# A decoder block in fp32 on one Trainium2 core: a new hand-written order of steps on every engine, new users of the PSUM banks, and 17 constant matrix products in place of 44

## The chip, the cores and the metric

The kernel runs on one core of a Trainium2 chip. The metric is the device time of one execution in microseconds (us), as the median of a few runs. The engines are PE (TensorE, matrix products; PEld is its weight load), DVE (VectorE), ACT (ScalarE), POOL (GpSimd) and SP (SyncE, which here issues all DMAs). They run side by side, each takes its own instructions in the order of the program, and they wait for one another on semaphores.

## What is computed

Four batches of 512 tokens with 128 features go through three residual stages:

```python
x = x + _L0_attn_ref(_layernorm(x), gamma)     # softmax(-gamma * |yi - yj|^2) @ y
x = x + _L0_xattn_ref(_layernorm(x), ctx, ctx, ...)   # 16 heads of 8, 154 keys, a bias linear in the distance
x = x + _L0_ffn_ref(_layernorm(x), ...)        # router: the best 2 of 8 experts, each 128x128
```

## The kernel before, in words

**Steps.** The work is cut into named steps. `name:b.k` is part k of batch b. Each engine's part of a step is a small function: `keys`, `maxima` and so on in the block of that engine. The functions wait on semaphores for what they read.

- Stage 1, a batch: DVE takes `stats1` (L981, L984), POOL turns a variance into a factor (`rstd1`: L695, L697; one call for batch 0, one for batches 1 to 3), DVE writes `y1` (L989), PE turns it (`y1T`, L1249: four 128x128 transposes, the "turned block"), ACT copies it to SBUF. POOL makes the squared norms (`squares`, L705 to L720, again batch 0 and then batches 1 to 3), PE turns them (`sqT`), ACT copies. PE forms four blocks of distances (`dist`, two fp32 instructions of 512 columns, L1263, and a bf16 one, L1266). DVE takes the row maximum (L1005), ACT clips (L851), DVE finishes `rowmax`, ACT takes the exponential (`soft`, L857), PE turns it (`probs`, L1214), ACT copies, and PE multiplies (`self`, L1279). DVE adds it to the residual and takes the next statistics (`gather`: L1019, L1023, L981, L984).
- Stage 2: `rstd2` (POOL), `y2` (DVE, L989), `y2T` and `query` (PE, L1286 and L1294, copied by ACT), `split` (a query in three bf16 pieces, three instructions; batch 0 on DVE, the others on POOL), then `qout` and `qin`: DMAs to DRAM and back into `qs`. The keys go the same way once: `keys` (ACT L871; DVE L1043 to L1049), `kout`, `kin`. `maxima` are 22 groups a batch: PE forms scores of three heads (L1316), DVE takes the maxima (L1091). `mcat` (DVE), `mT` (PE, ACT), `mout` and `min` (DMA) bring them back as three more rows of `qs`. `scores` (PE L1344, L1340; ACT exponential L919) are 20 a batch, `values` (PE L1371, L1367), `divide` (PE, DVE L1122, L1124), `aoT`, `wo` (PE L1390; DVE L1132 and the third statistics). `key_values` and `tail_values` write the values of all batches into `vm` and `vt`, which POOL clears first (`zeros`, L679 to L687).
- Stage 3: `rstd3`, `y3` (L989), `y3T`, `route` (PE L1404; DVE L1150 to L1166), `mask` (PE, ACT), masked tokens (`select`: batch 0 on POOL, L816, eight instructions, from `mask_all`, which comes over `eout` and `ein`; the others on DVE, L1186, from a product on PE, `spread`, L1421), `experts` (PE L1440) and `store`.

**Order.** The dictionary `ORDER` (L60) writes out by hand, for each engine, the list of its steps; `walk` (L238) goes through it. So an engine that waits in a step holds up all that is behind it in its list. Batches overlap: while DVE reduces `maxima` of batch 1, PE already works on `scores` of batch 0.

**Banks.** `TURNS` (L173) lists, for each of the eight PSUM banks, its users in order. Before a step writes, `turn` (L1204) lets PE wait until the user ahead of it in the list has been read.

**Constant products.** `WARM` (L232) gives numbers of products (L1210, 128x512 bf16 of a tile of ones, their results never read) that `turn` issues after its own wait and ahead of a step: 28 ahead of `y1T:0.0`, 4 ahead of `sqT:0.0`, 2 ahead of `probs:0.0`, 3 ahead of `y1T:3.0`, 2 ahead of `maxima:0.0`, 4 ahead of `probs:3.0`, 1 ahead of `scores:0.0`: 44 in all.

```python
for _ in range(WARM.get(f"{name}:{b}.{k}", 0)):
    mm(at(name, b, k)[:, :], idle[:, 0:P], idle[:, :], start=True, stop=True)
```

## Time and profile before

| what | us |
|---|---|
| median of 3 runs | 182.98 |
| the runs | 182.98, 184.85, 182.34 |
| span of the profiled execution, first to last instruction | 182.3 |
| busy in it: PE, PEld, DVE, ACT, POOL | 173.4, 123.6, 150.5, 105.8, 60.7 |

The profiled execution is one of its own; its time is its span and next to nothing around it, 0.04 us under the fastest of the runs shown and 0.7 us under their median. A row of the timeline gives the start, the duration, the engine, the line, the operation, output and inputs, shapes and a count, and in brackets the idle time of the engine before it with what ended it. Durations of PE overlap, since matmuls are pipelined: how far two starts lie apart tells more than one duration.

### The profile page before, as it was taken

How to read it: one execution, taken by the hardware profiler on the slowest of the kernel's cores; microseconds unless marked ns; L12 is line 12 of the kernel's file. 1: busy time of each engine (PE TensorE's matmuls, PEld its weight loads, DVE VectorE, ACT ScalarE, POOL GpSimd, SP SyncE). 2: the span in 40 equal slices, each digit the busy share in tenths (PEclk: the TensorE clock that was granted, in tenths of full speed). 3: DMA queues.
4: the chain of work that ended last, by engine and by line, in shares of the span. 5: the costliest groups of instructions: out<-in, count | busy, mean ns of one | idle time of the engine just before them, and what ended most of it. 6: DMA issues, size and time to landing. Idle time of an engine off the chain costs nothing.

```text
span 182.3 us, 4382 instructions
## 1 busy us (share of the span) xinstructions
PE 173.4 (95%) x1514; PEld 123.6 (68%) x1514; DVE 150.5 (83%) x433; ACT 105.8 (58%) x219; POOL 60.7 (33%) x123
## 2 busy tenths in 40 slices
...
GB/s 99 335 153 0 4 213 50 176 103 192 79 162 162 156 161 129 159 125 92 198 130 62 14 7 12 8 5 50 192 4 0 4 58 2 16 45 0 32 0 86
DMA packets 20003, 15.84 MB, mean 87 GB/s; under 512 B 1621, under 2 KB 18133, under 8 KB 19833
## 3 DMA queue, kind: packets, MB, share of 16 engines
...
q8 instruction: 12, 0.20, 0.5%
...
## 4 chain that ended last, share of the span: by engine, by line
PE 72%; DVE 19%; issue 3%; ACT 3%; POOL 1%; ACTq 0%; DVEq 0%
PE bank L1440 15%; DVE nm L1091 9%; PE bank L1371 8%; PE bank L1344 7%; PE bank L1316 6%; PE bank L1214 6%; PE bank L1263 6%; PE bank L1210 5%; PE bank L1279 4%; DVE y L989 3%; PE bank L1421 3%; PE bank L1340 2%; PE bank L1367 2%; ACT w L857 2%; PE bank L1390 2%
## 5 line engine op out<-in xcount | busy, mean ns | idle before, releaser
L1091 DVE TENSOR_REDUCE nm<-bank 128x3 f32<-128x462 f32 (+1 forms) x88 | 48.6, 614 | 0.8 <-PE bank L1316 0.6
L919 ACT ACTIVATE pt<-bank 128x512 f32<-128x512 f32 x80 | 43.3, 604 | 3.8 <-PE bank L1344 2.7
L1440 PE MATMUL bank<-ewT,ym 128*128 128x128 f32 x256 | 32.5, 277 | 0.0
L1440 PEld LDWEIGHTS bank<-ewT,ym 128*128 128x128 f32 x256 | 30.3, 192 | 0.2
L1316 PE MATMUL bank<-ks,qs 99*128 99x308 bf16 (+1 forms) x170 | 25.2, 262 | 0.0
L1344 PE MATMUL bank<-qs,ks 105*128 105x256 bf16 (+1 forms) x96 | 21.6, 309 | 0.0
L1316 PEld LDWEIGHTS bank<-ks,qs 99*128 99x128 bf16 x170 | 15.1, 98 | 8.3 <-DVE nm L1091 2.2
L1186 DVE TENSOR_TENSOR ym<-bank,y3T 128x512 f32<-128x512 f32 x24 | 15.1, 684 | 4.9 <-PE bank L1421 4.9
L798 POOL TENSOR_SCALAR ve<-mv 128x2 f32<-128x2 f32 (+1 forms) x6 | 1.3, 210 | 50.2 <-DVE mv L984 50.0
L1371 PE MATMUL bank<-pt,vm 128*32 128x256 f32 (+1 forms) x192 | 17.3, 456 | 0.0
L1263 PE MATMUL bank<-y1Tg,y1T 128*128 128x512 f32 x32 | 16.6, 601 | 0.3 <-ACT y1Tg L837 0.3
L989 DVE TENSOR_SCALAR y<-xs,mv,rs 128x128 f32<-128x128 f32 x48 | 16.2, 390 | 0.7 <-POOL rs L772 0.4
L1279 PE MATMUL bank<-y,pT 128*128 128x128 f32 x128 | 16.5, 278 | 0.2
L1279 PEld LDWEIGHTS bank<-y,pT 128*128 128x128 f32 x128 | 15.4, 191 | 1.2 <-DVE xs L1023 0.5
L1210 PE MATMUL bank<-idle 128*128 128x512 bf16 x44 | 13.6, 459 | 2.2 <-DVE idle L972 1.5
L851 ACT ACTIVATE w<-bank,snsq,sgn 128x512 f32<-128x512 f32 x16 | 12.3, 774 | 5.2 <-DVE rm L1005 5.2
L1005 DVE TENSOR_REDUCE rm<-bank 128x1 f32<-128x512 f32 x16 | 10.6, 681 | 4.8 <-PE bank L1266 4.8
L857 ACT ACTIVATE w<-w,nrb,sgn 128x512 f32<-128x512 f32 x16 | 12.9, 811 | 2.9 <-DVE nrb L1014 2.9
L824 ACT ACTIVATE maskT<-bank 128x256 bf16<-128x256 bf16 (+1 forms) x6 | 2.6, 454 | 19.6 <-PE bank L1440 14.0
L1344 PEld LDWEIGHTS bank<-qs,ks 105*128 105x128 bf16 x96 | 8.6, 97 | 7.5 <-issue 4.0
L981 DVE BATCH_NORM_STATS2 st<-xs 128x6 f32<-128x128 f32 x48 | 11.0, 282 | 1.1 <-DMA xs<-in_x_dram 0.6
L824 ACT ACTIVATE pT<-bank 128x512 f32<-128x512 f32 x16 | 9.6, 602 | 2.1 <-PE bank L1214 1.9
...
## 6 DMA issues: line engine op xcount, KB each, us to landing
...
```

The source lines that it names most:

```text
L857: nc.scalar.activation(w[b][:, t, :], w[b][:, t, :], ACT.Exp, bias=nrb[b][:, t:t + 1], scale=sgn[:, :], accum_out=den[b][:, t:t + 1]).then ...
L919: nc.scalar.activation(pt[:, n % RING, :], at("scores", b, i)[:, :], ACT.Exp).then_inc(exps, 1)
L989: v.tensor_scalar(y[:, t, :], src[:, t, :], mv[:, t, 0:1], rs[:, t:t + 1], ALU.subtract, ALU.mult).then_inc(s, 1)
L1091: v.tensor_reduce(nm[b][:, n:n + heads], at("maxima", b, g)[:, 0:heads * J].rearrange("p (s j) -> p s j", s=heads), AX.X, ALU.max, negate= ...
L1186: v.tensor_tensor(ym[:, e:e + per, c], masks, y3T[b][:, c].unsqueeze(1).broadcast_to([P, per, n]), ALU.mult).then_inc(masked_last, 1)
L1210: mm(at(name, b, k)[:, :], idle[:, 0:P], idle[:, :], start=True, stop=True)
L1263: mm(at("dist", b, t)[:, :], y1T[b][:, tile(t)], y1Tg[b][:, :], start=True, stop=False)
L1279: last = mm(at("self", b, p)[:, tile(t)], pT[b][:, t, u, :], y1[b][:, u, :], start=(u == 0), stop=(u == T - 1))
L1316: last = mm(at("maxima", b, g)[:, at_ * J:(at_ + heads) * J], qs[b][0:MAXROW, a, tile(t)], ks[b][0:MAXROW, a, s:s + heads, 0:J], start=Tru ...
L1344: last = mm(bank_[:, :], ks[b][0:TOP, h // 2, h % 2, 0:JM], qs[b][0:TOP, h // 2, c], start=True, stop=True)
L1371: last = mm(dst, vm[:, b, h, :], e, start=(r == 0), stop=(r == ROUNDS - 1), skip_group_check=True)
L1440: last = mm(at("experts", b, p)[:, tile(t)], ym[:, e, tile(t)], ewT[:, e, :], start=False, stop=(e == E - 1), skip_group_check=True)
```

## The change

Only `ORDER`, `TURNS` and `WARM` change. The steps are the same ones, as many on each engine, with the same instructions. The core of the diff, each part cut:

```diff
     "sync": """
-        x:0.0 gamma:0.0 x:1.0 x:2.0 k_rows:0.0 cols:0.0 x:3.0 context:0.0 weights:0.0 experts:0.0 k_rows:1.0
...
+        x:0.0 gamma:0.0 x:1.0 k_rows:0.0 k_rows:1.0 k_rows:2.0 k_rows:3.0 context:0.0 cols:0.0 experts:0.0 x:2.0 x:3.0
+        weights:0.0 q_rows:0.0 kout:0.0 kout:1.0 kin:0.0 kout:2.0 kin:1.0 kout:3.0 kin:2.0 kin:3.0 qout:0.0 qout:0.1
...
     "gpsimd": """
-        setup:0.0 gamma:0.0 rstd1:0.0 squares:0.0 bias:0.0 rstd1:1.0 weights:0.0 zeros:0.0 squares:1.0
-        rstd2:0.0 y1g:1.0 rstd2:0.1 y1g:2.0 x1b:0.0 rstd2:1.0 rstd2:1.1 y1g:3.0 split:1.0 x1b:1.0 split:1.1
...
+        zeros:0.0 setup:0.0 rstd1:0.0 gamma:0.0 squares:0.0 bias:0.0 weights:0.0 expert_bias:0.0 rstd1:1.0 squares:1.0
+        y1g:1.0 rstd2:0.0 y1g:2.0 rstd2:0.1 x1b:0.0 rstd2:1.0 rstd2:1.1 x1b:1.0 y1g:3.0 split:1.0 split:1.1 rstd2:2.0
...
     "scalar": """
+        table:0.0 y1T:0.0 sqT:0.0 dist:0.0 dist:0.1 dist:0.2 keys:0.0 soft:0.0 soft:0.1 probs:0.0 keys:0.1 probs:0.1
+        soft:0.2 dist:0.3 y1T:1.0 soft:0.3 sqT:1.0 probs:0.2 sqT:2.0 probs:0.3 dist:1.0 y2T:0.0 y1T:2.0 dist:1.1
+        dist:1.2 sqT:3.0 dist:1.3 y2T:0.1 soft:1.0 query:0.0 soft:1.1 query:0.1 probs:1.0 soft:1.2 soft:1.3 probs:1.1
...
     "vector": """
-        dist:0.3 rowmax:0.0 y1:1.0 keys:0.0 key_values:0.0 gather:0.0 key_values:0.1 key_values:0.2
-        key_values:0.3 y2:0.0 gather:0.1 y1:2.0 dist:1.0 y2:0.1 split:0.0 dist:1.1 dist:1.2 dist:1.3 rowmax:1.0
-        keys:0.1 split:0.1 dist:2.0 dist:2.1 dist:2.2 gather:1.0 dist:2.3 rowmax:2.0 y2:1.0 gather:1.1 y1:3.0
...
+        rowmax:0.0 keys:0.0 y1:1.0 keys:0.1 gather:0.0 key_values:0.0 dist:1.0 key_values:0.1 y2:0.0 key_values:0.2
+        y1:2.0 gather:0.1 dist:1.1 dist:1.2 key_values:0.3 dist:1.3 y2:0.1 rowmax:1.0 dist:2.0 tail_values:0.0
+        dist:2.1 split:0.0 dist:2.2 split:0.1 dist:2.3 rowmax:2.0 gather:1.0 gather:1.1 y2:1.0 y1:3.0 maxima:0.0
...
+        maxima:3.16 y3:0.0 maxima:3.17 maxima:3.18 maxima:3.19 maxima:3.20 divide:2.0 divide:2.1 maxima:3.21 mcat:3.1
+        route:0.0 divide:2.2 y3:1.0 wo:2.0 divide:2.3 y3:2.0 route:1.0 divide:3.0 wo:2.1 divide:3.1 wo:3.0 y3:2.1
...
     "tensor": """
-        scores:3.17 experts:0.1 experts:0.2 y3T:2.0 scores:3.18 wo:3.0 mask:1.0 scores:3.19 experts:0.3
...
+        start:0.0 y1T:0.0 sqT:0.0 dist:0.0 dist:0.1 dist:0.2 dist:0.3 keys:0.0 keys:0.1 key_values:0.0 probs:0.0
+        tail_values:0.0 probs:0.1 self:0.0 y1T:1.0 self:0.1 probs:0.2 sqT:1.0 sqT:2.0 sqT:3.0 probs:0.3 dist:1.0
+        self:0.2 self:0.3 y2T:0.0 dist:1.1 y1T:2.0 dist:1.2 dist:1.3 dist:2.0 query:0.0 y2T:0.1 dist:2.1 dist:2.2
+        query:0.1 probs:1.0 probs:1.1 dist:2.3 self:1.0 probs:1.2 probs:1.3 self:1.1 self:1.2 self:1.3 maxima:0.0
...
+        scores:3.12 scores:3.13 scores:3.14 values:3.3 scores:3.15 values:3.4 values:3.5 values:3.6 mask:1.0
+        experts:0.0 scores:3.16 scores:3.17 experts:0.1 experts:0.2 scores:3.18 scores:3.19 divide:3.1 experts:0.3
...
 WARM = {
-    "y1T:0.0": 28, "sqT:0.0": 4, "probs:0.0": 2, "y1T:3.0": 3, "maxima:0.0": 2, "probs:3.0": 4,
-    "scores:0.0": 1,
+    "y1T:0.0": 17,
 }
```

In `TURNS` each of the eight lists is written anew; the first users of each bank stay `y1T:0.0`, `sqT:0.0`, `dist:0.0` to `dist:0.3`, `kp:0.0` and `kp:0.1`. In the middle of the lists, `mcat:0.0` stands behind `maxima:1.0` and `y2:2.0` on DVE, where it stood ahead of `maxima:1.0`; `wo:1.0` stands ahead of `maxima:3.16`, where it stood behind `route:0.0`.

## Rows read from the trace of the kernel before

**Rows 1.** The page: busy time, share of the span, instructions

```profile
PE 173.4 (95%) x1514; PEld 123.6 (68%) x1514; DVE 150.5 (83%) x433; ACT 105.8 (58%) x219; POOL 60.7 (33%) x123
```

**Rows 2.** Busy time by stretches: stretch, length, engines, granted clock, DMA share, GB/s

```profile
10.48:13.78 3.30, 3.03 (x17) 1.80 (x16) 0.00 (x0) 1.67 (x3) 3.14 (x6) 1.00 0.12 47
...
45.96:62.88 16.92, 16.65 (x140) 11.90 (x140) 16.78 (x39) 10.13 (x23) 6.55 (x11) 1.00 0.49 131
...
74.23:119.00 44.77, 44.77 (x449) 26.65 (x450) 42.40 (x111) 36.70 (x75) 11.97 (x24) 1.00 0.28 77
...
140.40:182.30 41.90, 38.52 (x346) 35.56 (x346) 28.75 (x79) 5.03 (x13) 2.77 (x6) 1.00 0.08 26
```

**Rows 3.** The timeline: constant products on PE and their weight loads

```profile
1.50 9.13 PE L1210 MATMUL bank<-idle 128*128 128x512 bf16 x28 [1.50 <-DVE idle L972]
...
7.03 0.15 PEld L1210 LDWEIGHTS bank<-idle 128*128 128x128 bf16 x1 [0.28 <-issue]
...
7.46 2.69 PEld L1210 LDWEIGHTS bank<-idle 128*128 128x128 bf16 x13 [0.28 <-issue]
...
46.04 0.82 PE L1210 MATMUL bank<-idle 128*128 128x512 bf16 x3 [0.68 <-DVE y L989]
```

**Rows 4.** The timeline of the head, POOL, DVE, PE and ACT

```profile
5.35 1.04 POOL L697 TENSOR_TENSOR rs<-ve,minus_half 128x4 f32<-128x4 f32 x1
...
6.86 1.08 DVE L989 TENSOR_SCALAR y<-xs,mv,rs 128x128 f32<-128x128 f32 x4
...
10.48 0.60 PE L1249 MATMUL bank<-ident,y 128*128 128x128 f32 x4
...
12.20 0.59 ACT L824 ACTIVATE sqT<-bank 3x512 bf16<-3x512 bf16 x1
...
12.43 1.10 PE L1263 MATMUL bank<-y1Tg,y1T 128*128 128x512 f32 x2 [0.27 <-ACT y1Tg L837]
```

**Rows 5.** POOL's stretches: setup, squares:0.0, rstd1:1.0, zeros, squares:1.0, expert_bias

```profile
0.78:2.15 1.37, 1.12 (x7) 1.00 0.00 0
6.46:9.10 2.64, 2.06 (x9) 1.00 1.02 355
10.39:12.97 2.58, 2.50 (x3) 1.00 0.19 73
13.99:17.90 3.91, 3.62 (x10) 1.00 0.00 0
17.86:21.95 4.09, 3.52 (x10) 1.00 0.01 4
76.01:80.21 4.20, 3.64 (x11) 1.00 0.17 45
```

**Rows 6.** The timeline: one POOL cast of few elements, alone and beside DVE

```profile
8.35 0.20 POOL L716 CAST sqp<-nsr 128x4 bf16<-128x4 f32 x1
...
19.71 0.80 DVE L1045 TENSOR_TENSOR ym<-ym,mask_all 128x616 f32<-128x616 f32 x1
19.81 0.80 POOL L716 CAST sqp<-nsr 128x12 bf16<-128x12 f32 x1
```

**Rows 7.** The timelines of DVE and PE ahead of the first maxima

```profile
40.39 0.61 DVE L1023 SCALAR_TENSOR_TENSOR xs<-bank,rd,xs 128x128 f32<-128x128 f32 x2 [0.74 <-PE bank L1279]
...
43.79 1.35 PE L1316 MATMUL bank<-ks,qs 99*128 99x308 bf16 x12
```

**Rows 8.** The timeline of the late stretch, PE, DVE and POOL

```profile
122.96 0.40 PE L1214 MATMUL bank<-ident,maskp 128*128 128x128 bf16 x4
...
130.65 9.57 POOL L816 TENSOR_TENSOR ym<-mask_all,y3T 128x512 f32<-128x512 bf16 x8 [3.77 <-DMA mask_all<-e_scratch]
...
132.91 2.36 DVE L989 TENSOR_SCALAR y<-xs,mv,rs 128x128 f32<-128x128 f32 x2
...
135.29 1.11 PE L1440 MATMUL bank<-ewT,ym 128*128 128x128 f32 x8
...
140.43 0.38 PE L1214 MATMUL bank<-ident,maskp 128*128 128x128 bf16 x4 [0.92 <-DVE maskp L1166]
```

More of the change, by code:

```diff
@@ L77 @@
+        y1g:1.0 rstd2:0.0 y1g:2.0 rstd2:0.1 x1b:0.0 rstd2:1.0 rstd2:1.1 x1b:1.0 y1g:3.0 split:1.0 split:1.1 rstd2:2.0
+        split:2.0 rstd2:2.1 x1b:2.0 rstd2:3.0 split:2.1 rstd2:3.1 x1b:3.0 split:3.0 split:3.1 rstd3:0.0 rstd3:1.0
+        rstd3:2.0 select:0.0 select:0.1 select:0.2 select:0.3 select:0.4 select:0.5 select:0.6 select:0.7 rstd3:2.1
+        rstd3:3.0 rstd3:3.1
     """,
     "scalar": """
-        table:0.0 y1T:0.0 sqT:0.0 dist:0.0 dist:0.1 dist:0.2 keys:0.0 soft:0.0 soft:0.1 probs:0.0 probs:0.1
@@ L99 @@
+        scores:3.19 aoT:3.0 y3T:2.0 mask:1.0 y3T:2.1 values:3.2 values:3.3 aoT:3.1 mask:2.0 mask:2.1 y3T:3.0 y3T:3.1
+        mask:3.0 mask:3.1
     """,
     "vector": """
[L101 to L104 removed]
@@ L221 @@
-    """,
-    """
-        kp:0.1 dist:1.1 probs:1.0 probs:1.2 maxima:0.0 query:1.0 y2T:1.1 maxima:0.14 probs:2.3 probs:3.0
-        self:3.0 self:3.1 maxima:2.2 y2T:3.1 query:3.1 scores:1.2 maxima:2.16 scores:1.11 maxima:2.20
-        maxima:3.2 maxima:3.6 scores:2.1 scores:2.5 scores:2.8 maxima:3.16 scores:2.15 maxima:3.21 scores:3.0
-        mask:0.0 pv:2.3 scores:3.11 scores:3.15 aoT:3.0 wo:3.0 route:2.0 spread:2.0 spread:2.4 route:3.1
-        spread:3.3
+        y1T:0.0 vp:0.0 dist:2.1 y2T:1.0 query:1.0 maxima:0.10 probs:2.2 maxima:0.21 probs:3.1 maxima:1.5
@@ new lines @@
+        scores:0.0 scores:0.4 maxima:1.14 maxima:1.17 scores:0.15 divide:0.0 maxima:2.5 scores:1.0 maxima:2.12
+        maxima:2.15 maxima:2.19 scores:1.15 aoT:0.0 maxima:3.8 maxima:3.12 wo:0.0 wo:1.0 maxima:3.19
+        scores:2.17 aoT:2.0 y3T:1.0 aoT:2.1 scores:3.12 mask:1.0 spread:1.1 experts:1.0 route:3.0 spread:2.7
+        spread:3.4
+    """,
+    """
+        sqT:0.0 probs:0.0 probs:0.2 self:0.1 dist:2.0 y1T:3.0 maxima:0.5 self:2.0 y2T:2.0 query:2.0 maxima:1.1
+        probs:3.2 maxima:1.8 scores:0.7 scores:0.10 y2T:3.1 maxima:1.21 scores:0.19 query:3.1 scores:1.1
+        maxima:2.14 maxima:2.17 maxima:2.21 divide:1.0 maxima:3.7 maxima:3.10 pv:2.0 scores:2.13 scores:2.15
+        maxima:3.21 scores:3.2 pv:3.0 scores:3.13 scores:3.16 divide:3.1 route:2.0 mask:2.0 spread:2.3
+        experts:2.1 spread:3.6
@@ new lines @@
+    """,
+    """
+        dist:0.2 self:0.0 y2T:0.0 dist:1.3 probs:1.0 probs:1.3 probs:2.0 maxima:0.7 dist:3.1 maxima:0.15
+        maxima:0.20 probs:3.0 probs:3.3 self:3.1 maxima:1.13 maxima:1.16 scores:0.13 maxima:2.0 maxima:2.3
+        maxima:2.8 scores:1.3 scores:1.7 scores:1.11 scores:1.12 scores:1.14 scores:1.18 maxima:3.5 scores:2.2
+        maxima:3.13 scores:2.7 scores:2.11 maxima:3.20 scores:2.19 mT:3.1 wo:2.0 route:1.0 scores:3.11
+        scores:3.15 scores:3.18 wo:3.0 spread:1.0 spread:1.4 y3T:3.0 spread:2.5 spread:3.0 experts:3.0
```

219 lines of the change are left out of this document (94 added, 125 removed).

## The prediction

> **What bounds the kernel now.** I read the page's busy times first. PE is busy 173.4 of 182.3 us, DVE 150.5 [rows 1], so two engines could each be the limit, and the next view, busy time by stretches, has to say where. From 45.96 to 62.88 (the maxima of batch 0 up to their last) DVE is busy 16.78 of 16.92 us; from 74.23 to 119.00 PE is busy throughout, while DVE has 42.40 of 44.77; from 140.40 on DVE has slack (28.75 of 41.90) and PE has the experts to work through [rows 2]. The reader is to see a kernel that is bound by DVE up to about 70 us and by PE behind that. A new order can win only what these two now wait. Third, the timeline of the head: DVE has written y1 at 7.94 (6.86 + 1.08), but PE turns it at 10.48, since 28 constant products are ahead of it [rows 3, 4]. From there the chain goes through ACT to the first distance product at 12.43.
>
> **Part 1, the products ahead of the turned block.** The weight loads tell their pace: those at 7.03 and 7.46 are 0.43 us apart, and the 13 from 7.46 on take 2.69 us, 0.215 from start to start [rows 3]. So 14 products run at 0.43 (1.50 to 7.46) and 14 at 0.215. 512 columns in 0.43 us are the 1.2 GHz level and in 0.215 the 2.4 GHz level; the granted clock reads 1.00 in each stretch of [rows 2], which is the 2.4 GHz level. Seventeen products take 14 x 0.43 + 3 x 0.215 = 6.7 us and end at 8.2. That alone would bring the turned block forward by 2.3 us.
>
> **Part 2, POOL's head.** It doesn't, because zeros now stands first on POOL. From [rows 5]: zeros 3.9 us from 0.78 to 4.7; setup 1.4 to 6.1; rstd1:0.0 about 1.3 to 7.4 (now its last instruction ends at 6.39 and y1 starts at 6.86 [rows 4]), y1 then starts near 7.5, and takes 1.1 us to 8.6; the turned block done near 9.0. Gamma follows, 0.95 us (five small instructions, an estimate from the 0.2 us that such a one takes in [rows 6]), to 8.4; squares:0.0 2.6 to 11.05, where it now ends at 9.10. On PE sqT:0.0 is ahead of dist:0.0 and waits for it: turned at 11.65, and dist:0.0 starts there, not at 12.43. The copy of sqT (0.59 us [rows 4]) ends at 12.3, before the bf16 product wants it. So the head gains 0.75 us. Bounds: if the memsets of zeros were held up by DVE's own in the first 4 us as the cast in [rows 6] is (0.80 in place of 0.20), the loss is up to 2 us more, so the head is between -0.75 and +1.25; I take -0.75, since the setup memsets of POOL run beside one of DVE's at no loss (1.12 busy in 1.37 us [rows 5]).
>
> The Trainium skill (SBUF — State Buffer, Who interferes with whom) says that a DVE instruction with two SBUF inputs contends with a GpSimd one that reads SBUF, and that one with a single input outside the 2-port modes doesn't. The cast beside a two-input DVE instruction agrees. By the rule zeros runs at full pace beside DVE's memsets, which is the end of the range that I take.
>
> **Part 3, up to the first maxima.** POOL goes on: bias 0.6, weights 1.1, expert_bias 4.2 (now at 76 us), rstd1:1.0 2.6, so to 19.5, and squares:1.0, 4.1, to 23.7 in place of 21.95 [rows 5]. ACT's list has sqT:1.0 ahead of probs:0.2, so the copy of probs:0.2 and self:0.2 wait for it. DVE finishes rowmax:0.0 near 17.0 but waits for ACT's keys:0.0 (about 17.9), then has keys:0.0 (2.7), y1:1.0 (1.1), keys:0.1 (2.7), gather:0.0 (2.4) and small ones, and reaches the end of y2:0.0 at 28.7. Counted in work, the list of before has as much behind it at 28.7 (gather:0.1 and y1:2.0 in place of keys:0.1 and dist:1.0, 3.3 us on either side). So the 0.75 us are given back: +0.75. Bound: 0 to +1.5.
>
> From 28.7 I add DVE's steps in their order by the durations that they have now: dist:1.3 ends at 34.4, rowmax:1.0 35.4, tail_values 37.2, split:0.0 39.0, split:0.1 40.8, rowmax:2.0 41.9. Gather:1.0 needs self:1.1, which needs ACT's probs:1.1, and that stands behind soft:1.2 and soft:1.3: ACT, from rowmax:1.0, y2T:0.1, four exponentials of 0.9, two queries of 0.84 and two copies of 0.6, gives it at 42.0, PE's product ends at 43.0. DVE waits 1.1 us, where it now waits 0.74 [rows 7]. Maxima:0.0 then starts at 47.8. Now it starts at 45.96, and tail_values (1.2 us), which is now behind it, is ahead of it; the net is +0.65 us. The queries of batch 0 leave split:0.1 at 40.8, 3.0 us later than now, and so PE's first maxima product, now at 43.79 [rows 7], can't come before 46.8: PE stands idle some 2 us, but DVE isn't ready before 47.8, and PE has slack in this stretch. Cost on the path 0; if DVE were earlier, it would be up to 1 us.
>
> **Part 4, the 16 products further on.** At 0.215 us they are 3.45 us of PE's time. Those ahead of sqT:0.0 end when ACT is still copying y1T (dist:0.0 waits for ACT, 0.27 us, at 12.43 [rows 4]); the six ahead of probs:0.0 and probs:3.0 lie in the wait for an exponential. Those ahead of y1T:3.0, maxima:0.0 and scores:0.0 (six, 1.3 us) do push PE's next step, the first by 0.66 us (46.04 to 46.70 [rows 3]), but in the stretch where DVE is busy 16.78 of 16.92 us. Value 0; bound -1.3.
>
> **Part 5, the middle.** Mcat:0.0 comes behind maxima:1.0 and y2:2.0 and ends at 67.3 in place of 64.3; scores:0.0 then has its rows at about 74.3, now 71.4. PE's list has 2.0 us more work ahead of scores:0.0, so PE arrives with little to wait, 0.9 us behind its present state. That is the 0.65 again, within my error; nothing is added. Then PE works without a wait as now.
>
> **Part 6, the late stretch.** Mask:1.0 now waits 0.92 us for DVE [rows 8]: beside POOL's eight select instructions (9.57 us from 130.65) y3:2.0 takes 2.36 us for two instructions, where four of the same kind take 1.08 in [rows 4], and route:1.0 behind it is drawn out too. In the new list wo:1.0 is done earlier (2.0 us), route:1.0 runs near 130.3 to 132.5, and PE reaches mask:0.0 at 126.6, so select:0.0, 7.7 us behind mask:0.0 as now (122.96 to 130.65 [rows 8]), starts at 134.3, behind route:1.0. The wait at mask:1.0 goes: -1.1 with its issue. But PE reaches experts:0.0 at 135.1, and select feeds it every 1.2 us until 143.9, when experts:0.7 is due at 143.8: +0.2.
>
> **Part 7, what I haven't followed.** Of PE's 395 steps I followed some 80. Today's list has few waits behind 74; the new one has as many places for them. Between 0 and 4 us; I take +1.0, near the 1.1 us that the one such wait costs now.
>
> Sum: 182.3 - 0.75 + 0.75 + 0.65 + 0 - 1.1 + 0.2 + 1.0 = 183.05 us of span. The median stands 0.7 above the profiled span: **183.7 us**, no change that could be measured (2% is about what a measurement of this kernel tells from none).
>
> **Rivals.**
> *PE fills its waits* (faster). PE's present waits before 74 are the only reserve. If the head's 0.75 stays, the six products are worth their 1.3, mask:1.0 its 1.1, and the new order fills 1.5 us of the waits like the 0.68 at 46.04 [rows 3]: 182.98 - 4.65 = 178.3. For it: PE is at its limit behind 74. Against: before 70 DVE sets the pace, and its list holds the same work with 0.14 us of idle in 16.92.
> *POOL feeds the experts too late* (slower). One mechanism: batch 0's experts can't run before select, and select not before mask:0.0. Now select:0.0 ends at 131.8 and PE takes experts:0.0 at about 135.1 (its products from 135.29 [rows 8]), 3.3 us of slack; in the new list nearly none is left. Each microsecond that route:0.0 on DVE comes after 126.6 goes straight to the end. With DVE 3 us late (part 2's bound and part 7) and the eight selects drawn out from 1.16 to 1.34 us: 183.7 - 1.0 + 3 + 1.4 = 187.1. It decides from a mask:0.0 behind 129.5.
> *The clock falls in the head.* PE has no work from about 9.0 to 11.1, where now it has products (3.03 busy in 3.30 us, clock 1.00 [rows 2]). Now 6 us of products at the lower level do 3 us of work; the same once more would cost 3 us on the distance products, less what PE waits for anyway: 186.0. The Trainium skill (TensorE: Matmul & The Clock Gate, HAM oscillation) describes a kernel whose clock falls in each wait between two bursts of products; if this gap were one of those, the time would be this rival's 186.0. No row of this trace has such a gap.
>
> **Chances.** Forecast 0.50, its own range 181 to 186.5; filling 0.19; POOL late 0.22; clock 0.09 (half of it beyond 186.6). Faster by over 2% 0.19, within 0.54, slower 0.27. The range 178.5 to 188.0 takes in the rivals and leaves out about 0.15.
>
> **What would show it.** Right: y1T:0.0 at 8.6, dist:0.0 at 11.6 to 11.8, DVE's first maxima at 47 to 48.5, scores:0.0 near 74, no wait at mask:1.0, select:0.0 near 134. Wrong: a first maxima before 46, or a PE that waits more than 2 us between 75 and 140; weight loads 0.2 us long or distance products over 1.9 us apart after 11 would mean the clock.

## The result, and the profile after

The changed kernel takes **191.97 us** (median of 4 runs, 189.24 to 192.59). The kernel before took 183.03 us beside it; by the medians of all four runs the ratio is 1.049. Ratios and intervals in this document leave out executions over 1.5% above the fastest of their kernel, and go here by 191.81 and 189.24 us alone: 1.039, 1.028 to 1.050. It is slower either way, where no change was forecast. The profiled execution (191.81 us) has a span of 190.1 us and a granted clock of 0.964 in the mean, where it was 1.00 before. Two more executions had 0.964 (192.14 and 192.59 us); the fastest, 189.24 us, had 0.982.

The page after: PE does the same work, less 27 constant products, in a longer span, and the row of the clock has a 6 in three places.

```profile
PE 169.4 (89%) x1483; PEld 124.1 (65%) x1487; DVE 147.2 (77%) x433; ACT 104.6 (55%) x219; POOL 61.5 (32%) x123
...
PE   6659879985599999699959999999997999999894
...
PEclk9969999999669999999996999999999999999999
```

Busy time by stretches, after (stretch, length, PE, PEld, DVE, ACT, POOL, granted clock, DMA share, GB/s). These answer to [rows 2], but cut where the clock changes:

```profile
11.05:14.47 3.42, 3.04 (x8) 1.68 (x9) 2.45 (x17) 0.59 (x1) 2.91 (x11) 0.50 0.52 173
14.47:48.60 34.13, 28.46 (x199) 20.24 (x199) 29.50 (x90) 28.30 (x58) 16.27 (x29) 1.00 0.56 163
48.60:55.43 6.83, 5.61 (x29) 4.86 (x30) 3.90 (x8) 2.45 (x6) 1.96 (x2) 0.50 0.00 1
55.43:99.80 44.37, 40.26 (x318) 27.07 (x318) 39.96 (x103) 28.53 (x61) 16.51 (x28) 1.00 0.37 102
99.80:103.21 3.41, 3.41 (x17) 1.62 (x20) 2.87 (x10) 3.03 (x7) 0.00 (x0) 0.50 0.40 115
103.21:190.10 86.89, 82.42 (x900) 66.20 (x901) 62.49 (x182) 39.02 (x85) 14.98 (x20) 1.00 0.09 29
```

So TensorE runs at its 1.2 GHz level for 13.66 us and at 2.4 GHz otherwise. What PE did before each fall is in its timeline (start, length, engine, line, instruction, operands, count, idle before and what ended it), which answers to [rows 3, 4, 7]:

```profile
8.00 1.00 PE L1242 MATMUL bank<-ident,y 128*128 128x128 f32 x4 [1.32 <-DVE y L982]
11.43 0.59 PE L1207 MATMUL bank<-ident,sqp 128*128 128x128 bf16 x4 [2.42 <-POOL sqp L713]
11.81 2.02 PE L1256 MATMUL bank<-y1Tg,y1T 128*128 128x512 f32 x2
...
49.82 0.55 PE L1309 MATMUL bank<-ks,qs 99*128 99x308 bf16 x2 [4.35 <-DMA qs<-q_scratch]
...
78.57 0.59 PE L1337 MATMUL bank<-qs,ks 105*128 105x512 bf16 x2 [1.43 <-DMA qs<-m_scratch]
...
98.69 0.38 PE L1337 MATMUL bank<-qs,ks 105*128 105x512 bf16 x1 [2.10 <-DMA qs<-m_scratch]
```

Each fall comes behind a wait: 2.42 us for `squares:0.0`, 4.35 us for the first batch's queries on their way through memory, 2.10 us for the maxima's rows on the same way. The wait of 1.43 us ahead of `scores:0.0` had none. Behind the first, the two distance instructions take 2.02 us, where [rows 4] has 1.10.

The first maxima come 6.0 us later than in [rows 7] on PE (49.82 against 43.79). DVE's timeline shows the two splits of the queries back to back, and then DVE waiting in its turn:

```profile
39.22 0.42 DVE L1073 TENSOR_TENSOR qr<-qf,qpart 128x256 f32<-128x256 f32 x1
...
41.72 0.43 DVE L1077 TENSOR_TENSOR qpart<-qr,qpart 128x256 bf16<-128x256 f32 x1
...
50.40 0.64 DVE L1084 TENSOR_REDUCE nm<-bank 128x3 f32<-128x462 f32 x1 [1.90 <-PE bank L1309]
```

The late stretch, answering to [rows 8], went as forecast: no wait at `mask:1.0`, and POOL's `select` feeds the experts late by about a microsecond.

```profile
142.51 0.40 PE L1207 MATMUL bank<-ident,maskp 128*128 128x128 bf16 x4
...
144.19 1.16 PE L1433 MATMUL bank<-ewT,ym 128*128 128x128 f32 x8 [1.07 <-POOL ym L809]
```

### The profile page after: what moved, and what is told of

Read it like the earlier page. It is cut to its first block, busy times and chain, and to the rows that moved or that the text cites. A ratio compares the mean times of both kernels' runs of the same rounds, so it can differ in the third digit from the quotient of the medians.

```text
span 190.1 us, 4327 instructions
## 1 busy us (share of the span) xinstructions
PE 169.4 (89%) x1483; PEld 124.1 (65%) x1487; DVE 147.2 (77%) x433; ACT 104.6 (55%) x219; POOL 61.5 (32%) x123
## 4 chain that ended last, share of the span: by engine, by line
PE 55%; DMA 16%; POOL 9%; issue 5%; DVE 4%; SPq 3%; ACT 2%; ACTq 0%; POOLq 0%
PE bank L1433 15%; PE bank L1309 8%; PE bank L1337 6%; PE bank L1364 5%; DMA q_scratch<-qpart 5%; PE bank L1207 4%; DMA m_scratch<-mT 4%; PE bank L1414 3%; SPq L550 3%; DMA qs<-m_scratch 3%; DMA mask_all<-e_scratch 2%; PE bank L1272 2%; PE bank L1256 2%; PE bank L1360 2%; DMA qs<-q_scratch 2%
## 5 line engine op out<-in xcount | busy, mean ns | idle before, releaser
L1084 DVE TENSOR_REDUCE nm<-bank 128x3 f32<-128x462 f32 (+1 forms) x88 | 49.4, 616 | 7.3 <-PE bank L1309 7.2
L912 ACT ACTIVATE pt<-bank 128x512 f32<-128x512 f32 x80 | 42.2, 608 | 13.1 <-PE bank L1337 10.9
L1433 PE MATMUL bank<-ewT,ym 128*128 128x128 f32 x256 | 31.4, 277 | 1.1 <-POOL ym L809 1.1
L1309 PE MATMUL bank<-ks,qs 99*128 99x308 bf16 (+1 forms) x170 | 24.5, 281 | 4.3 <-DMA qs<-q_scratch 4.3
L1337 PE MATMUL bank<-qs,ks 105*128 105x256 bf16 (+1 forms) x96 | 19.3, 319 | 3.5 <-DMA qs<-m_scratch 3.5
L1256 PE MATMUL bank<-y1Tg,y1T 128*128 128x512 f32 x32 | 17.7, 635 | 0.0
L1364 PE MATMUL bank<-pt,vm 128*32 128x256 f32 (+1 forms) x192 | 16.3, 454 | 0.0
L982 DVE TENSOR_SCALAR y<-xs,mv,rs 128x128 f32<-128x128 f32 x48 | 13.8, 343 | 3.1 <-POOL rs L800 1.9
L1207 PE MATMUL bank<-ident,w 128*128 128x128 f32 x64 | 9.8, 285 | 1.4 <-ACT w L850 1.3
L809 POOL TENSOR_TENSOR ym<-mask_all,y3T 128x512 f32<-128x512 bf16 x8 | 9.0, 1161 | 5.4 <-DMA mask_all<-e_scratch 5.4
## 6 DMA issues: line engine op xcount, KB each, us to landing
q_scratch<-qpart SPq DMA_DIRECT2D x8, 192.0 KB, 2.1
qs<-q_scratch SPq DMA_DIRECT2D x8, 192.0 KB, 3.5
```

The source lines that it names most:

```text
L912: nc.scalar.activation(pt[:, n % RING, :], at("scores", b, i)[:, :], ACT.Exp).then_inc(exps, 1)
L982: v.tensor_scalar(y[:, t, :], src[:, t, :], mv[:, t, 0:1], rs[:, t:t + 1], ALU.subtract, ALU.mult).then_inc(s, 1)
L1084: v.tensor_reduce(nm[b][:, n:n + heads], at("maxima", b, g)[:, 0:heads * J].rearrange("p (s j) -> p s j", s=heads), AX.X, ALU.max, negate= ...
L1207: last = nc.tensor.transpose(dst[:, tile(t)], src(t), id_[:, :])
L1256: mm(at("dist", b, t)[:, :], y1T[b][:, tile(t)], y1Tg[b][:, :], start=True, stop=False)
L1309: last = mm(at("maxima", b, g)[:, at_ * J:(at_ + heads) * J], qs[b][0:MAXROW, a, tile(t)], ks[b][0:MAXROW, a, s:s + heads, 0:J], start=Tru ...
```

## The experiments

The medians are of all executions, 4 to 12 a run. All ratios are to the kernel before, run beside (182.7 to 183.0 us). `WARM` and the orders are those of the front. Where a diff shows parts of an order, a line is a part of its list.

| run | median us | ratio, 95% |
|---|---|---|
| after_warm | 186.91 | 1.017 to 1.025 |
| before_bare | 181.41 | 0.989 to 0.996 |
| after_zeros | 193.26 | 1.052 to 1.064 |
| after_queries | 193.7 | 1.049 to 1.064 |
| head_before_tail_after | 204.77 | 1.108 to 1.127 |
| head_after_tail_before | 186.54 | 1.013 to 1.027 |
| before_zeros_first | 184.54 | 1.007 to 1.015 |
| before_late_queries | 191.34 | 1.039 to 1.055 |
| after_products_maxima | 189.2 (186.58 to 192.71) | 1.013 to 1.035 |
| after_old_head | 187.13 | 1.016 to 1.032 |
| after_early_queries | 188.65 | 1.025 to 1.039 |
| after_both | 187.75 | 1.018 to 1.034 |
| after_early_queries_2 | 186.85 | 1.017 to 1.026 |
| after_both_2 | 187.3 | 1.019 to 1.029 |
| after_both_bare | 188.01 | 1.012 to 1.028 |
| before_17keep | 181.51 | 0.990 to 0.996 |
| after_three_repairs | 188.99 | 1.030 to 1.038 |
| before_late_after | 183.59 | 1.001 to 1.008 |

### What the clock costs: after_warm, after_products_maxima

```diff
 WARM = {
-    "y1T:0.0": 17,
+    "y1T:0.0": 17, "sqT:0.0": 10, "probs:0.0": 3, "sqT:1.0": 5, "maxima:0.0": 20, "scores:0.0": 7, "scores:1.0": 10,
 }
```

after_products_maxima has `"y1T:0.0": 17, "maxima:0.0": 20` alone.

> The changed kernel with constant products put into its own gaps: 10 ahead of sqT:0.0, 3 ahead of probs:0.0, 5 ahead of sqT:1.0, 20 ahead of maxima:0.0, 7 ahead of scores:0.0, 10 ahead of scores:1.0, the order unchanged. Theory A (the clock is the main cost: low for 13.7 us in three falls): no fall, the distance products of batch 0 start at 11.8 and end 1.5 us earlier, the first eight maxima are paced by DVE, and the time falls by 4 to 6 us to about 186.5. Theory B (the waits of the new order are the cost, and the clock's falls lie in time that is lost anyway): within 1 us of 191.9, with the clock high.

> after with 20 products ahead of maxima:0.0 and no others beside the 17. after has its clock at half for 3.4 us from 11.05, 6.8 us from 48.6 and 3.4 us from 99.8; holding all three up was worth 5.1 us. Theory A (each fall costs what lies on the path in it): the middle one is half of the low time and lies in a stretch where PE also waits for DVE, so 2 to 3.4 us: 189.2 us (188.5 to 190), with the falls at 11 and near 100 still there. Rival (one fall is as good as another, the order of the batches' later steps takes it up): 191 or more.

Measured: 186.91 us (186.68 to 187.06) and 189.2 us. The stretches of after_warm that answer to the three falls:

```profile
11.00:14.50 3.50, 3.23 (x13) 1.53 (x13) 2.20 (x15) 0.59 (x1) 2.95 (x12) 1.00 0.60 210
48.60:55.40 6.80, 6.75 (x49) 5.08 (x49) 5.93 (x12) 3.68 (x11) 3.15 (x5) 1.00 0.10 29
99.80:103.20 3.40, 3.40 (x46) 1.58 (x42) 2.36 (x5) 2.77 (x7) 0.00 (x0) 1.00 0.09 25
```

With 55 products more, the kernel is 5.1 us faster (191.97 - 186.91), and so are the profiled spans (190.1 - 185.0). Order and banks are the same and the clock stays up, so 5.1 us is what the falls cost, less what the 55 products themselves may hold up: 13.66 us at half speed do the work of 6.83 us, and most of the difference lay on the path. after_products_maxima gets 2.8 of the 5.1 us by the medians, with a spread of 6 us. Its trace (188.08 us) still has the fall near 11 (page: a 6 in that slice), but none behind its waits for the maxima's rows (2.18 us at 77.00, 2.00 us at 97.04); so not all of the 2.8 need be the middle fall's.

The spread is more telling than the median, since each execution has its own granted clock. Over such a span a mean of 0.991 is about 3.4 us at the lower level, 0.982 about 6.7 and 0.964 about 13.7.

| kernel | granted clock: us of its executions |
|---|---|
| changed kernel | 0.982: 189.24; 0.964: 191.81, 192.14, 192.59 |
| after_products_maxima | 1.000: 186.58; 0.991: 188.08; 0.982: 190.32; 0.972: 192.71 |
| after_both_bare (below) | 1.000: 185.78; 0.991: 187.48; 0.982: 188.53, 188.73 |
| before_zeros_first (below) | 1.000: 184.50; 0.989 to 0.991: eight, 184.18 to 184.73; 0.981: 186.14 |

In after_products_maxima each further 3.4 us of low clock goes with 1.5 to 2.4 us more. Its execution without a fall takes 186.58 us, level with after_warm (186.91), which has 35 products more: what the products give is the clock. In before_zeros_first the first 3.4 us cost nothing that shows. So the price of a fall depends on where it lies. The executions without a trace don't tell which wait brought the fall, or whether that wait was longer in them.

### Which products the order of before needs: before_bare, before_17keep

before_bare is the kernel before with `WARM = {"y1T:0.0": 17}`; before_17keep has 17 in place of 28 and the 16 later ones kept.

> The kernel before with the table of constant products of the changed one: 17 ahead of the turned block and none later, its order unchanged. Theory A1 (the products hold the clock up wherever the order waits): one or two falls and 184 to 187 us. Theory B1 (in this order PE has hardly a wait, so the clock needs no products, and the order alone makes the falls): no fall, and 181 to 183 us, since the head starts up to 2 us earlier.

> The order of before with 17 products ahead of y1T:0.0 and its 16 later ones kept: against before it prices the 11 products of the head, against before_bare (181.41) the 16 later ones. Prediction's part 4 (the 16 are worth nothing): 181.4 to 181.6. Rival (its bound, 1.3 us, PE is pushed by them): 182.2 to 182.7, so that the head's 11 are worth nothing and the later ones all of what before_bare gained.

Measured: 181.41 and 181.51 us. So leaving out eleven products of the head gains 1.3 us (182.72 to 181.41, 182.83 to 181.51), and the 16 later ones are worth nothing, as part 4 had it. In this order the clock stays up without them. Waits of before_bare on PE behind the first product:

```profile
PE bank L1213 <- ACT w L856: 2.9, 4, 1.4
...
PE bank L1248 <- DVE y L988: 0.9, 1, 0.9
PE bank L1213 <- POOL sqp L719: 0.9, 1, 0.9
```

(microseconds in total, times, longest). Fewer products alone made the kernel faster than both: all the loss comes with the new order, and with its clock held up that is 186.91 - 181.41 = 5.5 us. The new order with the 44 products of before is not tried.

### Where the order loses it: exchanging halves

Both kernels take one order on all engines up to the last of batch 0's maxima and the other behind it. In short:

```diff
 # head_after_tail_before
-    the order and banks of before, up to maxima:0.21 (SP: up to qin:1.5)
+    the order and banks of after, up to there, products as in after_warm
```

> The other half: order of after up to maxima:0.21 with products in its gaps that keep the clock up (17, 10, 3, 5 and 20 ahead of y1T:0.0, sqT:0.0, probs:0.0, sqT:1.0 and maxima:0.0), order of before behind it. Theory O: 186.5 us (185.5 to 188), as after_warm or a little above. Rival L: 182 to 183.5.

> Order of before on every engine up to the last block of the first batch's maxima (PE and DVE up to maxima:0.21, ACT up to probs:2.3, SP up to kin:2.0, POOL up to expert_bias:0.0), order and bank users of after behind it; only the 17 products ahead of y1T:0.0. Theory O (what the new order costs lies ahead of the first batch's last maxima, and its later part is worth what it was predicted to be, about -0.5 to -1.5 us): 180.5 us, 179.5 to 181.8. Rival L (the later part costs time too: after waits 1.6 and 2.3 us for the maxima's round trip ahead of scores:0.0 and scores:1.0): 183 us or more.

Measured: 186.54 us, level with after_warm. With before's order behind batch 0's maxima nothing is won, so the loss can't lie in what is behind them alone; much of the lag is there by then: `maxima:0.0` on PE is at 49.6, against 41.4 in before_bare. The other half says nothing: at its seam SP waits 10 us in `qout` of batch 2, with the maxima's rows behind it, and PE waits 8.6 us. I draw nothing from its 204.77 us.

### What delays the head: before_zeros_first, before_late_queries

Each puts one part of the new order into before_bare.

```diff
 "gpsimd" of before_zeros_first
-        setup:0.0 gamma:0.0 rstd1:0.0 squares:0.0 bias:0.0 rstd1:1.0 weights:0.0 zeros:0.0 squares:1.0
+        zeros:0.0 setup:0.0 rstd1:0.0 gamma:0.0 squares:0.0 bias:0.0 weights:0.0 expert_bias:0.0 rstd1:1.0 squares:1.0
 "vector" of before_late_queries
-        dist:1.0 y2:0.1 split:0.0 dist:1.1 dist:1.2 dist:1.3 rowmax:1.0 keys:0.1 split:0.1 dist:2.0 dist:2.1 dist:2.2
+        dist:1.0 dist:1.1 dist:1.2 dist:1.3 y2:0.1 rowmax:1.0 keys:0.1 dist:2.0 dist:2.1 split:0.0 dist:2.2 split:0.1
```

> before_bare with after's order on POOL up to squares:1.0 (zeros first, expert_bias ahead of rstd1:1.0), nothing else. after_warm has dist:0.0 1.9 us later than before_bare (11.65 against 9.73) and sqT:1.0 2.9 us later. Theory P (that lag goes on to the end): 183.5 us (182.5 to 184.5) by the head's lag less what waits take up. Rival (the lag is taken up by the waits behind it, as the zeros then no longer stand ahead of squares:1.0): 181.4 +- 0.5. If the clock falls in the wait that is now longer ahead of sqT:0.0, 2 us more.

> before_bare with the first batch's query steps at after's places on PE, ACT and DVE (query:0.0, y2T:0.1, query:0.1, y2:0.1, split:0.0, split:0.1 behind dist:2.0 to dist:2.2; three of them take other banks). Theory Q (the first maxima wait for the round trip of the queries through memory, so later splits move them and all behind): split:0.1 ends 4 us later or more (35.6 in before_bare), the first maxima start on PE at 46 to 48 (41.4), the time is 184 to 186.5 us. Rival (PE does meanwhile what it does later in before, and gets it back): 181.4 to 182.4.

Measured: 184.54 and 191.34 us, so +3.1 and +9.9 over before_bare. PE's timelines (the first line is before_zeros_first, the others before_late_queries):

```profile
11.45 0.38 PE L1213 MATMUL bank<-ident,sqp 128*128 128x128 bf16 x4 [2.44 <-POOL sqp L719]
```

```profile
34.31 0.70 PE L1289 MATMUL bank<-y2T,wT 128*128 128x256 f32 x2 [3.29 <-ACT w L846]
...
50.29 2.47 PE L1311 MATMUL bank<-ks,qs 99*128 99x308 bf16 x12 [3.75 <-DMA qs<-q_scratch]
```

Zeros ahead of `squares:0.0` brings PE the same wait as in the changed kernel, and the clock falls behind it (8 and 8 on the page in the slices from 9.1 to 18.3 us). The late queries bring the wait ahead of the first maxima and the fall behind that, and a second pair near 34, where `query:0.0` waits for a bank that I gave it: 9.9 us is more than the late queries alone. Each part is enough to make the kernel slower. For the zeros it seems to be the later head more than the clock: the one execution of ten that kept its clock at 1.00 took 184.50 us, as long as the eight at 0.989 to 0.991 (184.18 to 184.73).

How the queries go their way through memory is in SP's timeline (its DMA issues). First before_bare:

```profile
27.32 1.92 SPq L556 DMA_DIRECT2D q_scratch<-qpart  x2
...
35.18 0.90 SPq L556 DMA_DIRECT2D q_scratch<-qpart  x2
36.12 2.70 SPq L556 DMA_DIRECT2D qs<-q_scratch  x4
```

and the changed kernel:

```profile
38.05 3.33 SPq L550 DMA_DIRECT2D q_scratch<-qpart  x4
41.42 0.68 SPq L550 DMA_DIRECT2D qs<-q_scratch  x1
42.14 1.11 SPq L550 DMA_DIRECT2D q_scratch<-qpart  x2
43.29 3.93 SPq L550 DMA_DIRECT2D qs<-q_scratch  x5
```

When the second split ends (35.6 and 42.15), before_bare has six DMAs to issue and the changed kernel seven, since in SP's new list `qin:0.1` stands behind `qout:0.4` and `qout:0.5`, where before has it ahead of them; the prediction didn't look at that. The last is issued at 47.2, 5.1 us behind the split's end, where before_bare needs 3.2 (35.6 to 38.8). From the split's end to PE's first maxima it is 7.7 us, in place of 5.8.

One DMA more is not the whole cause, and neither is how close together the splits are. before_late_queries has six left (behind three loads of `q_rows`), and takes 8.6 us (41.70 to 50.29). after_both has its splits 3.7 us apart and takes 7.4 (38.90 to 46.28). after_old_head has the list and the spacing of the changed kernel here, 1.7 us, and takes 8.8 (40.09 to 48.88), with these rows:

```profile
40.07 1.10 SPq L550 DMA_DIRECT2D q_scratch<-qpart  x2
41.22 4.77 SPq L550 DMA_DIRECT2D qs<-q_scratch  x5
```

```profile
48.88 0.36 PE L1309 MATMUL bank<-ks,qs 99*128 99x308 bf16 x2 [1.15 <-DMA qs<-q_scratch]
```

What sets the length of this way stays open.

### Repairs of the new order

after_zeros (no products) gives POOL the head of before; after_queries (no products) moves the first queries earlier. after_old_head (products as in after_warm) gives SP and POOL the head of before. after_early_queries moves the queries in another way, after_both joins the two. The cores of after_old_head and after_early_queries:

```diff
 "sync"
-        x:0.0 gamma:0.0 x:1.0 k_rows:0.0 k_rows:1.0 k_rows:2.0 k_rows:3.0 context:0.0 cols:0.0 experts:0.0 x:2.0 x:3.0
-        weights:0.0 q_rows:0.0
+        x:0.0 gamma:0.0 x:1.0 x:2.0 k_rows:0.0 cols:0.0 x:3.0 context:0.0 weights:0.0 experts:0.0 k_rows:1.0 k_rows:2.0
+        k_rows:3.0 q_rows:0.0
 "tensor"
-        dist:1.2 dist:1.3 dist:2.0 query:0.0 y2T:0.1 dist:2.1 dist:2.2 query:0.1 probs:1.0
+        dist:1.2 query:0.0 dist:1.3 y2T:0.1 dist:2.0 query:0.1 dist:2.1 dist:2.2 probs:1.0
```

> The changed kernel with POOL's head as before (zeros behind weights, expert_bias behind rstd2:3.0), all else unchanged. Theory C (the fall at 11 us comes of PE's 2.4 us wait for squares:0.0 behind zeros): squares:0.0 done by 9.3, PE's wait under 1 us, no fall in the head, dist:0.0 at about 10 to 10.5, squares:1.0 done by about 22 to 23 in place of 25.7; 2 to 3 us of it reach the end, 189 us, while the fall at 48.6 stays. Rival (the head is given back at the queries): the first maxima stay at 50 and the time within 1 us of 191.9.

> The changed kernel with the queries of batch 0 earlier on PE, ACT, DVE and SP (query:0.0 behind y1T:2.0, y2T:0.1 behind dist:1.2, query:0.1 behind dist:1.3, split:0.0 and 0.1 ahead of rowmax:1.0, kin:2.0 and kin:3.0 behind the queries of batch 0). Theory D (PE's 4.4 us wait for the queries' return, and the fall of the clock at 48.6 behind it, are the largest loss): PE waits under 1.5 us ahead of maxima:0.0, no fall there, maxima:0.0 on DVE near 47.5 and its eighth near 52 in place of 56.8, time 187 to 188. Rival (DVE would have been late anyway, since split and y2 displace its other steps): 190 to 192.

> after with the order of before on SP and POOL for the head (x:2.0 and x:3.0 ahead of the context, weights ahead of the expert weights; zeros behind weights, expert_bias late), and products in the gaps as in after_warm (3 in place of 10 ahead of sqT:0.0). Theory H (the head costs by two things that overlap: zeros ahead of squares:0.0, and the late loads of x:2 and x:3, for which DVE waits 3.3 us ahead of its reductions of dist:0.0; undoing one alone leaves the other): dist:0.0 at 9.8, probs:0.0 at 17.3, squares:1.0 ends by 21.6, the time is 185.0 us (184.5 to 186) against 186.9 of after_warm. Rival (the head's lag is taken up by the first maxima, which wait for the queries anyway): 186.5 to 187.

> after_warm with query:0.0, y2T:0.1 and query:0.1 up to 5 steps earlier on PE (no bank's order changed), their copies on ACT ahead of soft:1.0, split:0.0 and split:0.1 on DVE 2 to 3 steps earlier (split:0.0 ahead of dist:2.0), SP's kin:2 and kin:3 behind the queries; products in the gaps (6 ahead of maxima:0.0, 10 ahead of y1T:3.0). Theory D2 (what made the queries' round trip late is half of it; behind it DVE has its own list full up to 47.9): the first maxima on DVE start at 48.0 in place of 49.5 and the time is 185.3 us (184.5 to 186.2). Rival Q (the round trip is all of it): first maxima on DVE at 46 or before, 183.5. Rival (no gain, as PE or a bank holds them): 186.9.

> after_old_head and after_early_queries together, products as in the latter with 3 ahead of sqT:0.0. From the first maxima on PE to spread:3.0 after_warm takes 123.9 us and before_bare 126.4, so if the way up to the first maxima is repaired the rest of the new order is ahead. Theory: the two gains add up, first maxima on DVE at 46 to 46.5, time 183.4 us (182.3 to 184.5). If the head's repair is worth its full 2 us behind the queries and PE finds work for the rest: 181.5, level with before_bare. Rival (they overlap): 185.

Measured: 193.26, 193.7, 187.13, 188.65, 187.75: no gain came out as expected. In after_zeros `sqT:0.0` no longer waits long (PE at 9.3), but DVE reaches the reduction of `dist:0.0` late all the same, since ahead of it in its list stand the statistics of x:2, which SP now loads behind the keys' rows, the context and the expert weights: they wait 4.23 us. The changed kernel waits there too:

```profile
11.95 0.87 DVE L974 BATCH_NORM_STATS2 st<-xs 128x6 f32<-128x128 f32 x4 [3.33 <-DMA xs<-in_x_dram]
```

So two delays lie side by side in the head, and undoing one leaves the other; I had overlooked the second. after_old_head undoes both, and its second split ends 1.4 us earlier than in after_warm (40.09 against 41.53), but the longer way through memory takes that back: PE's first maxima are at 48.88, against 49.07. In after_queries `query:0.1` had to wait 2.9 us for its bank. In after_early_queries ten of my own products stood ahead of `y1T:3.0`, and DVE waited for the second group of maxima behind them:

```profile
49.17 0.64 DVE L1085 TENSOR_REDUCE nm<-bank 128x3 f32<-128x462 f32 x1 [0.38 <-PE bank L1310]
...
52.41 1.19 DVE L1085 TENSOR_REDUCE nm<-bank 128x3 f32<-128x462 f32 x2 [2.08 <-PE bank L1310]
```

That fault was mended in after_early_queries_2, with `split:0.1` also ahead of `tail_values:0.0` on DVE. after_both_bare is after_both_2 with the 17 products alone.

```diff
 "vector" of after_early_queries_2 and after_both_2
-        dist:1.3 y2:0.1 rowmax:1.0 dist:2.0 tail_values:0.0 dist:2.1 split:0.0 dist:2.2 split:0.1 dist:2.3
+        dist:1.3 y2:0.1 rowmax:1.0 split:0.0 dist:2.0 split:0.1 tail_values:0.0 dist:2.1 dist:2.2 dist:2.3
```

> after_early_queries with its own fault mended: 12 products ahead of maxima:0.0 and none ahead of y1T:3.0 (there they held back maxima:0.1, for which DVE waited 2.1 us), and split:0.1 now ahead of tail_values:0.0 and dist:2.1 on DVE. Theory D3 (behind 28 us DVE's list is full, so what decides the time of split:0.1 is what stands ahead of it on DVE): split:0.1 ends at 39.4 (41.5 in after_warm), PE's first maxima at 46 to 47, DVE's at 47.9, so -1.6 on the path: 185.3 us (184.6 to 186.2). Rival (the later waits for the memory round trips of m and of batch 1's queries take it back, as after_old_head's gain was): 186.7 to 187.2.

> The same with the head of before on SP and POOL. Theory (gains up to the first maxima go through to the end): DVE's first maxima at 46.2, 183.7 us (182.8 to 184.8). Rival (they are lost behind scores:0.0: after_both had its last block of batch 0's maxima 0.8 us before after_warm's and scores:1.0 2.2 us behind it): 186 to 187.5, with scores:1.0 not before 95.5.

> after_both_2 with only the 17 products ahead of y1T:0.0. after has three falls of the clock, behind waits of 2.6, 4.5 and 2.3 us on PE; with the head and the queries repaired those ahead of sqT:0.0 and maxima:0.0 are about 1.4 and 2 us. Theory (the falls come from the order's long waits and go with them): granted clock 0.985 or more and the time within 1.5 us of after_both_2. Rival (this order needs the products wherever it waits): clock 0.97 and 4 us or more above after_both_2.

Measured: 186.85, 187.3 and 188.01 us. The first maxima do move, and their last group on PE too: 63.85 in after_warm, 61.68 in after_both_2. But then `scores:1.0` is at 96.44, behind the 95.52 of after_warm: the 2.2 us that were won are lost again, and 0.9 more. Two rows of after_both_2, ahead of `scores:1.0` on PE and in the middle of batch 1's maxima on DVE:

```profile
96.44 0.39 PE L1337 MATMUL bank<-qs,ks 105*128 105x512 bf16 x1 [0.97 <-DMA qs<-m_scratch]
```

```profile
81.55 0.60 DVE L982 TENSOR_SCALAR y<-xs,mv,rs 128x128 f32<-128x128 f32 x2 [1.23 <-POOL rs L765]
```

PE waits for the rows of batch 1's maxima, though ten products stand ahead of the wait. From `scores:0.0` to `scores:1.0` it takes 23.3 us here, 20.0 in after_warm and 18.2 in before_bare, which has its PE busy throughout. So the rival held, in time and in `scores:1.0`: what is won ahead of batch 0's maxima is gone by this second wait. after_both_bare still lets the clock fall twice (mean 0.982), behind its waits for the rows of both batches:

```profile
73.96 0.59 PE L1337 MATMUL bank<-qs,ks 105*128 105x512 bf16 x2 [2.28 <-DVE nm L1084]
...
95.28 0.38 PE L1337 MATMUL bank<-qs,ks 105*128 105x512 bf16 x1 [1.74 <-DMA qs<-m_scratch]
```

With 17 products it is 4.0 us faster than the changed kernel, and 0.7 us from after_both_2. Its one execution with the clock at 1.00 took 185.78 us, less than any of after_both_2 (186.80 to 187.87), so the products that I put into the waits may well cost about a microsecond themselves. Its waits ahead of `sqT:0.0` and `maxima:0.0` are below 1 us and have no fall behind them: these two falls of the changed kernel went with the waits that the order made.

after_three_repairs attacks the second wait by moving `gather:3.1` and `y2:3.1` behind `mcat:1.0` on DVE, as before has them, with other banks for four steps and 3 products in place of 10 ahead of `scores:1.0`:

```diff
 "vector"
-        gather:3.0 maxima:1.8 maxima:1.9 gather:3.1 maxima:1.10 maxima:1.11 maxima:1.12 y2:3.0 maxima:1.13 y2:3.1
+        gather:3.0 maxima:1.8 maxima:1.9 maxima:1.10 maxima:1.11 maxima:1.12 y2:3.0 maxima:1.13
```

> after_both_2 with gather:3.1 and y2:3.1 on DVE behind mcat:1.0, as in before (now ahead of maxima:1.10 and maxima:1.14; in after_both_2 gather:3.1 takes 2.85 us from 74.41 and y2:3.1 is waited for, 1.23 us), y2T:3.1 and query:3.1 on PE and y2T:3.1 on ACT later in keeping, split:3.0 ahead of rstd2:3.1 on POOL; since self:3.1 then holds its bank longer, maxima:1.13, maxima:1.16, scores:0.13 and maxima:2.0 take other banks; 3 products in place of 10 ahead of scores:1.0. Theory M (this is the second place where the order of after is longer: from scores:0.0 to scores:1.0 it takes 20.0 to 23.3 us where before takes 18.0, and mcat:1.0 comes later by those two steps): mcat:1.0 ends by 84.5 (87.2), scores:1.0 by 93 (96.4), time 184.3 us (183.3 to 185.3). Rival (PE waits for the round trip of the queries of batch 2 or for banks instead): scores:1.0 at 95 or behind, 186.5 to 187.5.

Measured: 188.99 us, `scores:1.0` at 98.4: worse. DVE now waits for PE. As I read the lists, `self:3.1` keeps its bank longer and the maxima of batch 1 have one fewer; no run tries that by itself:

```profile
77.83 1.73 DVE L1085 TENSOR_REDUCE nm<-bank 128x3 f32<-128x462 f32 x3 [2.23 <-PE bank L1310]
```

An order and its bank users can't be changed one without the other. Which single step makes the stretch from `scores:0.0` to `scores:1.0` longer stays open.

### The late stretch: before_late_after

before_bare up to `scores:2.19`, and the order and banks of after behind it.

```diff
 # before_late_after
-    before's order behind scores:2.19 (DVE: behind maxima:3.21)
+    after's order there
```

> before_bare up to scores:2.19 (DVE up to maxima:3.21), and behind that the order and bank users of after. after_warm takes 62.9 us from scores:2.0 to spread:3.0 and before_bare 64.1; prediction's part 6 gave the late stretch of after 0.9 us less (no wait at mask:1.0). Theory: 180.3 us (179.8 to 180.9). Rival (the seam costs what it gains, or the gain of after_warm there came from work it had done before scores:2.0): 181.4 to 182.5.

Measured: 183.59 us, 2.2 us slower than before_bare. PE's timeline has two waits that before_bare doesn't have:

```profile
119.25 1.07 PE L1366 MATMUL bank<-pt,vm 128*32 128x256 f32 x16 [2.13 <-DVE ao L1119]
...
135.51 1.16 PE L1435 MATMUL bank<-ewT,ym 128*128 128x128 f32 x8 [1.21 <-POOL ym L811]
```

The first belongs to the seam. The second is POOL's `select` feeding `experts:0.0` late; it takes about what the missing wait at `mask:1.0` gives (0.8 us in before_bare). Four executions of the twelve also had a clock of 0.981 or 0.991 and took 184.8 to 185.1 us, a fifth 185.57. So the late stretch of the new order shows no gain here; what it is worth by itself the seam keeps open.

## Why the prediction was wrong

It said 183.7 us, and 191.97 were measured: 8.3 us more. The first term below is shown by a run. The two others are my working of the sum, and no run gives or takes them by themselves:

- **The clock: 5.1 us** (after against after_warm). This was the rival "the clock falls in the head", at a chance of 0.09 and a price of 2.3 us. The wait it named is there (2.42 us ahead of `sqT:0.0`), and the distance products show it. What the rival missed is that a falling clock isn't a matter of the head. The step that failed is in part 3: "PE stands idle some 2 us, but DVE isn't ready before 47.8, and PE has slack in this stretch. Cost on the path 0". The wait was 4.35 us, and the clock behind it was at half for 6.83 us, in which PE, which was said to have slack, had none (stretch from DVE's first maxima to the last of batch 0):

```profile
50.40:70.00 19.60, 19.55 (x125) 15.20 (x125) 17.43 (x40) 10.58 (x23) 7.82 (x13) 0.87 0.35 92
```

  Here an idle PE would have cost little only if its clock had stayed up. How the 5.1 us divide among the three falls isn't measured; by the executions of after_products_maxima 3.4 us of low clock go with 1.5 to 2.4.
- **The first maxima: 1.9 us of span.** after_warm has a span of 185.0, and the sum was 183.05. Part 3 had DVE's first maxima at 47.8; with the clock up they are at 49.47, 1.67 us later, held by PE, whose first maxima are at 49.07. `split:0.1` ends at 41.5, where I had 40.8. The term that was mis-sized is the way through memory: I took the 6.0 us of before and it took 7.5. That this lag is what the end is late by is the sum's reading and not shown: after_both_2 had DVE's first maxima at 47.29 and ended no earlier, since `scores:1.0` stayed late.
- **The yardstick: 1.0 us.** I set the time 0.7 us above the span, and wrote that the time of an execution is its span and next to nothing around it. That was wrong: in every execution of the result and the experiments, those of the kernel before too, it is 1.7 to 1.8 us above. So the profiled execution of before, with its span of 182.3, was by that one of 184.0 us, not the median. What it had too much was probably in the head, 28 products whose pace rose late (below): its first distance product is 2.70 us behind that of before_bare (12.43 against 9.73) and its span 2.5 us longer, where the medians are 1.3 us apart. I worked out the new head in absolute times, so that excess was no part of the new sum, and 1.7 was to be added to it, not 0.7.
- The rest, 0.3 us, is within the runs' spread.

Point by point. Parts 1 and 2 were close in their times: `squares:0.0` ends at 11.28 (forecast 11.05), `dist:0.0` starts at 11.81 (11.65); the 17 products ended at 6.7 and not at 8.2, which nothing waited for. But the head was never going to gain its 0.75 us: before_bare, with POOL's head as it was, starts `dist:0.0` at 9.73. What I counted as a gain against 12.43 was a loss of 2.1 us (11.81 against 9.73) against what the eleven dropped products alone bring, and before_zeros_first, which has zeros first too, is 3.1 us slower than before_bare. I also passed over SP's list: x:2 comes so late that DVE waits 3.33 us for it, with its first reduction behind that.

`squares:1.0` was forecast at 4.1 us to 23.7 and took 5.8 us to 25.7: several of its instructions run beside two-input instructions of DVE's `keys`, and take 0.8 in place of 0.2 to 0.4 us.

```profile
22.25 0.34 POOL L704 TENSOR_SCALAR snsq<-nsq,sgn 128x12 f32<-128x12 f32 x1
...
23.56 0.80 POOL L709 CAST sqp<-nsr 128x12 bf16<-128x12 f32 x1
```

The Trainium skill (SBUF — State Buffer, Who interferes with whom) states that a DVE instruction with two SBUF inputs contends with a GpSimd one that reads SBUF. This trace agrees: the 0.80 us cast runs beside a two-input instruction of 0.80 us. Zeros took its 3.9 us beside DVE's memsets, which have no inputs. I had used the rule for zeros and not for `squares:1.0`.

Part 4 was right, and before_17keep and before_bare show it (0.1 us between them). What it left out is that the new order has longer waits, in which products had a use (after_warm); whether those same 16 would have done isn't tried. Part 5 had `scores:0.0` at 74.3; it was 75.5 with the clock up and 78.57 as it is. "Then PE works without a wait as now" was wrong at `scores:1.0`, where PE waits 2.10 us for batch 1's rows. Part 6 was right: `select:0.0` starts 8.7 us behind `mask:0.0` (7.7 forecast), there is no wait at `mask:1.0`, and the experts wait about 1.1 us. "POOL feeds the experts too late" is thus real, but takes only back what `mask:1.0` gives. From `scores:0.0` to `spread:3.0` after_warm takes 97.5 us, before_bare 98.9: behind the first scores the new order is ahead, as I take it for what it did while PE waited earlier.
